# Two small groups of matmuls moved ahead of two large ones in the TensorE order of a slot-attention stage

## The reference

```
x = layernorm(x + mamba(x))                 # stage 1
x = layernorm(x + slot_attention(x, ctx))   # stage 2
x = layernorm(x + experts(x))               # stage 3: each token through one of 8 experts
```

```
for _ in range(3):
    sn = rmsnorm(slots, slot_norm_w)
    scores = (sn @ Wq.T) @ k_proj.T * SCALE       # [slots 128, context 77]
    attn = softmax(scores, axis=slots)
    attn = attn / (sum(attn, axis=context) + EPS)
    updates = attn @ v_proj
    slots = gru_cell(updates, slots)              # gates r, z, n
```

## Time and profile before

| what | value |
|---|---|
| median of 3 runs | 1726.81 us (1726.34 to 1732.19) |
| the profiled execution | 1726.34 us, span 1724.3 us |
| stage 2 in the span | about 944 to 1525 us; its beats from 963.8 to 1501 us |
| PE busy, whole span | 1490.1 us (86%) |
| DVE busy | 1290.3 us (75%) |
| ACT busy | 1080.9 us (63%) |
| POOL busy | 1199.8 us (70%) |
| mean granted PE clock | 0.93 of full speed |

### The profile page before, as it was taken

One profiled execution on the slowest core, in us unless ns is written; L12 is line 12 of the kernel. 1 busy time (PEld: TensorE's weight loads), 2 busy tenths in 40 slices (PEclk: granted clock), 3 DMA queues, 4 the chain that ended last, 5 costly groups with the idle time before them and its releaser, 6 DMA issues. The chain is left out here.

```text
span 1724.3 us, 21744 instructions
## 1 busy us (share of the span) xinstructions
PE 1490.1 (86%) x6178; PEld 887.3 (51%) x6178; DVE 1290.3 (75%) x2194; ACT 1080.9 (63%) x2151; POOL 1199.8 (70%) x863
## 2 busy tenths in 40 slices
PE   4888899888998889988885899999999999819994
PEld 1333334333433334333332577777777777619994
DVE  1999999999999999999992356566666666624542
ACT  3767777777777777777763566565666665404553
POOL 1799999999999999999994114446446445443665
PEclk8889999999999999999988999899999999959997
DMA  3445454454554445444441802113023000017771
GB/s 129 149 148 173 147 165 161 158 166 145 165 168 155 155 147 178 160 170 148 148 134 26 333 5 104 56 69 115 17 104 120 13 1 14 12 30 212 211 206 50
DMA packets 105848, 214.19 MB, mean 124 GB/s; under 512 B 12162, under 2 KB 56709, under 8 KB 105744
## 3 DMA queue, kind: packets, MB, share of 16 engines
q1 hardware_dynamic: 101200, 204.50, 36.9%
q0 software_dynamic: 4544, 8.47, 1.4%
HBM read 168.28 MB, written 45.56 MB: 124 GB/s over the span
## 5 line engine op out<-in xcount | busy, mean ns | idle before, releaser
L321 POOL TENSOR_TENSOR hc<-state,c_rows 128x1024 f32<-128x1024 f32 x256 | 599.0, 2360 | 42.3 <-DVE state L503 33.9
L606 PE MATMUL ps_y<-hc,ident 128*128 128x512 f32 x1024 | 515.0, 646 | 91.3 <-POOL hc L321 91.3
L503 DVE TENSOR_TENSOR_SCAN state<-ps_da,inp 128x512 f32<-128x512 f32 x512 | 591.6, 1205 | 0.0
L395 ACT ACTIVATE ps_da<-dt,a_neg 128x512 f32<-128x512 f32 x512 | 349.1, 688 | 172.0 <-DVE state L503 167.9
L606 PEld LDWEIGHTS ps_y<-hc,ident 128*128 128x128 f32 x1024 | 202.4, 203 | 382.1 <-issue 232.1
L492 DVE TENSOR_TENSOR inp<-dtx,ps_b 128x1024 f32<-128x1024 f32 x192 | 231.8, 1207 | 35.3 <-ACT ps_b L401 19.2
L918 POOL TENSOR_TENSOR rs<-ms,m_half 128x4 f32<-128x4 f32 x48 | 49.5, 1032 | 243.9 <-DVE ms L1144 243.8
L308 POOL TENSOR_TENSOR inp<-dtx,b_rows 128x1024 f32<-128x1024 f32 x64 | 150.9, 2358 | 0.1
L552 PE MATMUL ps_misc<-x1T,w_conv 128*128 128x512 f32 (+3 forms) x256 | 119.3, 611 | 23.7 <-ACT x1T L346 15.3
L401 ACT COPY ps_b<-b_rows 128x512 f32<-128x512 f32 x192 | 111.6, 581 | 26.3 <-DVE inp L492 24.5
L1056 ACT ACTIVATE ex<-sc,nmx 77x128 f32<-77x128 f32 x192 | 74.7, 390 | 74.0 <-DVE nmx L1153 74.0
(11 more groups left out here) (210 smaller groups left out, 2735.3 us busy)
## 6 DMA issues: line engine op xcount, KB each, us to landing
b_rows<-bc_rows SPq DMA_DIRECT2D x128, 512.0 KB, 4.9
c_rows<-bc_rows SPq DMA_DIRECT2D x128, 512.0 KB, 4.0
sorted_x<-pad_rows SPq DMA_DIRECT2D x8, 4160.0 KB, 13.4
w<-in_L_ffn_W SPq DMA_DIRECT2D x78, 256.0 KB
xrow<-sorted_x SPq DMA_DIRECT2D x39, 130.0 KB, 2.4
x_tok<-in_x SPq DMA_DIRECT2D x16, 256.0 KB, 4.5
ctx<-in_ctx SPq DMA_DIRECT2D x16, 154.0 KB
out_x<-orow,target POOLq DMA_INDIRECT x78
```

The source lines that it names most:

```text
L321: pool.tensor_tensor(hc[:, n % RING], state[:, n % RING], over_c(c_rows[:, slot, n % 2]), ALU.mult).then_inc(hc_ready, 1)
L395: act.activation(ps_da[u % DA_RING][:], dt[:, par, c], ACT.Exp, scale=a_neg[:, c, n:n + 1]).then_inc(da_ready, 1)
L503: dve.tensor_tensor_scan(state[:, n % RING, c], ps_da[u % DA_RING][:], inp[:, n % RING, c], 0.0, ALU.mult, ALU.add).then_inc(state_ready, 1)
L606: ins = pe.matmul(ps_y[:, c], ident[:], hc[:, n % RING, c], start=False, stop=n == NS - 1)
```

## The change

Only the order of four calls in TensorE's queue of stage 2 changes. `den` goes ahead of `gate_h` r, and `den_spread` goes ahead of `gate_h` z. `count` stays between them. No instruction is added or taken away, and the queues of the other engines are as before.

```diff
@@ -1403,12 +1403,12 @@
                 for name in u_names(beat, 0, first, last):
                     make_u(i, par, name, first, last)
                 gate_h(a, it, par, "hn", other, it2)
+                den(a, it)
                 gate_h(a, it, par, "r", other, it2)
-                den(a, it)
                 if beat in (4, 5) and not first:
                     count(beat - 4, i - 1, b, it2)
+                den_spread(a, it)
                 gate_h(a, it, par, "z", other, it2)
-                den_spread(a, it)
                 for name in u_names(beat, 1, first, last):
                     make_u(i, par, name, first, last)
                 after_this = following(beat, i, par, last)
```

## The result

The changed kernel takes 1772.64 us in the median of four runs (1766.69 to 1782.13) against 1726.96 us (1726.34 to 1732.19): a ratio of 1.026 with a 95% interval of 1.021 to 1.032, so 2.6% slower. I had forecast 1750 in a range of 1735 to 1762. The direction and the mechanism of the waits were right and the size was not: 23 us forecast, 45.7 measured. The profiled execution takes 1769.67 us against 1726.34, and that difference of 43.3 us is what the traces have to explain.

The account below looks back on a forecast made before the run. TensorE's queue was taken as close to the bound, each beat a ring from `rse` to the next. 3.1 us for each of seven pairs (21.7) plus 1.5 in pair 7 made 23.2, so 1750 us, range 1735 to 1762.

Parts of the forecast that it names:

- r loses its cover, PE waits for `rse`: TensorE's queue: r (0.86 us), free during the exponentials, now queues behind `den`, starting 0.97 us after `rse` ends (E).
- almost exact: Before the change, r ends at 1250.57 and `rse` at 1250.41, 0.06 to the load: r just fills TensorE's wait.
- `den_spread` gains nothing, as `rdn` holds it: TensorE's `den_spread` stays 2.09 us after `rse` ends, waiting for VectorE's `rdn`; in beats 4 and 5 `count` delays it.
- z behind `rdn` moves all that follows by 0.86: TensorE, after `den_spread`: z no longer fills the wait for `rdn`, so second unit, `ssq`, `scores`, `root_spread` move 0.86 us.
- GpSimd sets the end ... beats 4 and 5 together get +0.78: GpSimd's gapless queue from `ctx_r` to `rs` ends beat 5; it starts 0.78 us later, adding that per pair.
- TensorE's clock ... So I expect it full: Stage 2: TensorE, busy 91% with waits below 1 us each, was expected to keep its full granted clock.
- The rival with its chance of 0.07: New TensorE waits make the granted clock fall once per pair: 7 x 4.6 = 32 us on top, 1782; chance 0.07.
- The faster rival: Attention weights come sooner as `den_spread` moves up 0.86 us, TensorE's waits go: 1704, more likely 1715; chance 0.05.
- the share of 91%: TensorE's expected busy share in the new order: 64.2 of 70.5 us per pair.
- The range: 1735 to 1762: forecast with its bounds 1738 and 1760, two clock falls, and part of the case where much is hidden.

Follow-up runs that it names:

- e10: Kernel before the change, with the first 256 columns of product hn computed twice (0.43 us more TensorE work per beat): 1736.8 us, ratio 1.006.
- e2: Kernel before the change with only `den_spread` moved ahead of `gate_h` z, `den` left behind r: 1788.3 us, ratio 1.038.
- e4: Changed kernel, with GpSimd issuing two of beat 5's four scatter DMAs behind the next root instead of ahead: 1770.3 us, ratio 1.027.
- e5: Changed kernel, with two of beat 5's four scatter DMAs moved behind the next root and the next pair's residual add: 1761.1 us, ratio 1.022.
- e1: Kernel before the change with only `den` moved ahead of `gate_h` r, `den_spread` left behind z: 1760.8 us, ratio 1.020.
- e6: Changed kernel with both the two scatter DMAs moved behind the next pair's residual add and 256 columns of hn computed twice: 1742.7 us, ratio 1.011.
- e3: Changed kernel, with the first 256 columns of product hn computed twice inside the new wait for `rse`: 1766.4 us, ratio 1.023.
- e8: Changed kernel, with ScalarE's copy `load_h` of beat 4 put behind the sums of squares, starting GpSimd's chain sooner: 1752.0 us, ratio 1.018.

## Why the prediction was wrong in size

- **r loses its cover, PE waits for `rse`: right.** 0.81 us of wait in the beat shown, r at E + 0.97. That the cover was "almost exact" holds for the start of `den`, which e10's filler of 0.43 us pushed back by 0.31, but such a delay cost the beat 0.2 to 0.3 us in beats 1 and 2 and nothing in beat 0.
- **`den_spread` gains nothing, as `rdn` holds it: right.** It stays at E + 2.09 in the changed kernel and in e2.
- **z behind `rdn` moves all that follows by 0.86: right.** The root distances of beats 0 to 4 were forecast as 7.03, 7.03, 6.79, 7.01, 7.70, and are 7.02, 7.02, 6.74, 7.05, 7.78. In pair 7 the later beats are unchanged where the clock is full (beat 2: 10.79 us in both kernels).
- **Beat 5, "GpSimd sets the end ... beats 4 and 5 together get +0.78": mis-sized.** The mechanism was there (e4, e5), but I moved the chain of 9.85 us as a block and kept its length. It measured 11.13, since the shift brought its instructions beside others of VectorE; the two beats got 2.1 us together. That is 1.3 us in each of five pairs, 6 us. I should have looked which instructions the chain would meet after the shift.
- **"TensorE's clock ... So I expect it full": failed.** I put the clock at nothing, since pair 7 of the kernel before ran at full clock with PE busy 90%. The granted clock over the beats was 0.94 against 0.99 before, and it cost 14 us more than before in the profiled execution. PE's busy share was no guide: over pairs 1 to 6 PE is busy 92% of the time in e1 at a mean clock of 1.00, and 93% in the changed kernel at 0.96. The runs show that the waits matter: with the waits for `rse` partly filled and the long wait of beat 5 shortened (e6) no fall is left from pair 1 on, with only one of the two done (e3, e5) some falls are left. The rival with its chance of 0.07 named this cause, but not its size: most of the 14 us (8.5) came in pair 7 and not as one fall a pair, and the time came out as my forecast, plus the 6 us of beat 5, plus about half of what that rival added.
- **A wrong sum.** PE's busy times in the earlier trace rows add up to 65.20 us and not to 64.20, so 2.2 us of a pair were idle and not 3.2, and PE was busy 97% of it. The faster rival and the share of 91% rest on the wrong figure (by the right one it is 92.5%); the 1750 doesn't.
- **The range.** I let the clock widen it by two falls only (1762). Without the two terms above it would have come out right: a pair of the changed kernel without a cost from the clock takes 4.3 us more than before, and 3.0 without the longer chain, where I had 3.1.

What stays open: why some waits of the same length are followed by a fall and others aren't. e1, e5 and e8 have the same waits for `rse` as the changed kernel (0.47 to 0.81 us in pairs 1 to 6). In their profiled executions e1 has one fall in pairs 1 to 6, which cost almost nothing, e8 one, and e5 three pairs without any; e2, with waits of 0.85 to 0.99 behind `den` instead, has the most. The filler shows that the waits take part in it, and not which of them starts a fall. A profile was taken of only one execution of each kernel, so the places of the falls are those of one execution.

## What to carry to other kernels

When the order of an in-order queue changes, write the times of one period relative to the event that the next period hangs on; a product that filled a wait was free here, and behind the wait it cost up to its full length (0.86 us in beat 0). Before moving an instruction up, ask who waits for it: `den` had nobody, and `den_spread` was held by another engine. And shifting another engine's chain by half a microsecond can change its length and TensorE's clock, so a forecast for a queue that is 97% busy needs a term for both.

## What the runs showed of the hardware

- Instructions of GpSimd and VectorE stretched each other where they overlapped, `row`, `ids`, `df` and `nmx` to the end of the other's instruction: 0.19 to 0.64 us (`row` beside `df`), 1.03 to 1.59 (power beside `rh`), 0.69 to 1.15 (`df` beside `pn`), and a 77x4 instruction of VectorE from 0.17 to 1.18 beside a residual add on GpSimd. A shift of 0.5 us in e8 undid the first two and stretched `ids` to 0.78 us instead.
- More work made the kernel faster: 0.43 us of repeated products in each beat took the median from 1761.1 (e5) to 1742.7 us (e6), with the granted clock at 1.00 from pair 1 to pair 7, where it had fallen to half speed several times. In the kernel before, the same products made it slower (1736.8 against 1725.7, e10).
